# Attention slots in half slots: values of two key tiles per burst, paired products in pieces, gathers one by one, and the second SwiGLU product moved to GpSimd

## What is computed

```python
xn = _layernorm(x, axis=-1)
x = x + attn(xn) + ffn(xn)
# attn: holo_linear(x, basis, phase, amp): (x @ basis.T) @ (amp * cos(phase)).T, rank 32
#   q, k, v = holo_linear(xn), 16 heads of 16 columns; softmax(q k / 4) v; holo_linear again
# ffn: 8 experts with 352 hidden columns, the two best per token (softmax, renormalised, times 2.5)
#   silu(x @ wg) * (x @ wu) @ wd
#   plus a shared expert with 704 hidden columns on every token
```

## Time and profile before

| | |
|---|---|
| three timed runs | 1054.34, 1055.94, 1062.08 us; median 1055.94 |
| profiled execution | 1056.45 us, span 1054.6 us |
| mean granted clock of TensorE | 0.926 |
| busy over the span | TensorE 931.8 us (88%), VectorE 646.0 (61%), ScalarE 568.1 (54%), GpSimd 327.9 (31%) |

### The profile page before, as it was taken

One profiled execution on the slowest core, in us unless ns is written; L12 is line 12 of the kernel. 1 busy time (PEld: TensorE's weight loads), 2 busy tenths in 40 slices (PEclk: granted clock), 3 DMA queues, 4 the chain that ended last, 5 costly groups with the idle time before them and its releaser, 6 DMA issues.

```text
span 1054.6 us, 19404 instructions
## 1 busy us (share of the span) xinstructions
PE 931.8 (88%) x6519; PEld 624.2 (59%) x6520; DVE 646.0 (61%) x978; ACT 568.1 (54%) x892; POOL 327.9 (31%) x305
## 2 busy tenths in 40 slices
PE   5756999999999779898998998998997998998898
PEld 3446999999999624455454455444544544544546
DVE  7778644444434555765774874874875775785653
ACT  5756544444444335554663663663664664665563
POOL 2006422222222060351343253244235235135043
PEclk9856999999999856898998998998998999999899
DMA  9976454222222354445446545545465365453220
GB/s 317 377 253 191 137 164 115 73 71 70 70 70 66 94 146 127 124 119 147 126 117 174 151 111 166 147 129 142 133 154 154 108 169 134 138 122 77 48 63 21
DMA packets 94086, 140.02 MB, mean 133 GB/s; under 512 B 18200, under 2 KB 51488, under 8 KB 92992
## 3 DMA queue, kind: packets, MB, share of 16 engines
q1 hardware_dynamic: 87328, 121.25, 40.5%
q0 software_dynamic: 6480, 17.70, 5.7%
q10 hardware_dynamic: 208, 0.14, 0.0%
HBM read 79.24 MB, written 54.71 MB: 127 GB/s over the span
## 4 chain that ended last, share of the span: by engine, by line
PE 48%; issue 24%; POOL 11%; DVE 9%; ACT 3%; another core or an unknown queue 2%; DMA 2%; SPq 0%; POOLq 0%; ACTq 0%; DVEq 0%
PE bank L1253 7%; PE s_pair L1235 6%; PE st_pair L1235 6%; PE bank L1382 5%; PE bank L1444 4%; PE st_pair L1370 4%; POOL y_b L784 3%; PE bank L1348 3%; POOL h_T L767 3%; PE s_pair L1309 3%; DVE top L1773 2%; PE bank L1243 2%; PE bank L1218 2%; ACT prob L1031 1%
## 5 line engine op out<-in xcount | busy, mean ns | idle before, releaser
L1773 DVE TENSOR_REDUCE top<-s_pair 128x2 f32<-128x1024 f32 x252 | 308.5, 1224 | 144.0 <-PE s_pair L1309 122.7
L1031 ACT ACTIVATE prob<-st_pair 128x1024 f32<-128x1024 f32 x256 | 261.6, 1022 | 217.1 <-PE st_pair L1370 152.5
L767 POOL TENSOR_TENSOR h_T<-h_f,h_T 128x512 fp32r<-128x512 f32 x40 | 51.3, 1283 | 410.7 <-ACT h_T L1013 410.7
L1382 PE MATMUL bank<-prob,v_ones 128*32 128x512 f32 x1024 | 156.4, 637 | 4.6 <-issue 4.3
L745 POOL DMA_INDIRECT xg<-xn_rows,token_of x71 | 82.9, 1168 | 216.6 <-PE bank L1218 164.6
L1348 PE MATMUL bank<-xT_b,w_sh 64*128 64x512 f32 x960 | 129.5, 402 | 15.7 <-DVE h_f L1794 13.4
L1370 PE MATMUL st_pair<-q_rows,k_rows 50*128 50x512 f32 x512 | 126.3, 480 | 14.7 <-ACT prob L1031 7.5
L1309 PE MATMUL s_pair<-k_rows,q_rows 48*128 48x512 f32 x504 | 117.0, 450 | 14.4 <-DVE top L1773 7.4
L1370 PEld LDWEIGHTS st_pair<-q_rows,k_rows 50*128 50x128 f32 x512 | 51.0, 191 | 122.8 <-ACT prob L1031 78.0
L1348 PEld LDWEIGHTS bank<-xT_b,w_sh 64*128 64x128 f32 x960 | 91.1, 188 | 43.4 <-DVE h_f L1794 22.3
L1253 PE MATMUL bank<-w_exp,c_hT 128*128 (+1 forms) x639 | 94.2, 292 | 1.0 <-ACT c_y L957 1.0
(11 more groups left out here) (233 smaller groups left out, 1163.7 us busy)
## 6 DMA issues: line engine op xcount, KB each, us to landing
qk_rows<-qk_hi SPq DMA_DIRECT2D x56, 256.0 KB
q_rows<-qk_rows SPq DMA_DIRECT2D x64, 192.0 KB
k_rows<-qk_rows SPq DMA_DIRECT2D x56, 192.0 KB
expert_rows<-c_y SPq DMA_DIRECT2D x71, 128.0 KB, 1.7
xn_T_split<-x_T SPq DMA_DIRECT2D x8, 1024.0 KB, 6.5
xT_b<-xn_T_split SPq DMA_DIRECT2D x32, 256.0 KB
qk_rows<-qk_lo SPq DMA_DIRECT2D x28, 256.0 KB
x_all<-in_L_attn_x_dram SPq DMA_DIRECT2D x8, 512.0 KB, 8.1
```

The lines of the kernel that those rows point to most:

```text
L767: pool.tensor_tensor(h_T[0:m, LO, f, :], h_f[q % 2][0:m, :], h_T[0:m, HI, f, :].bitcast(F32), ALU.subtract).then_inc(p_h, 1)
L1031: act.activation(prob[kt % 2][:, 2 * jp:2 * jp + 2, :].rearrange("p j l -> p (j l)"), st_pair[:, :], ACT.Exp, scale=HD ** -0.5).then_inc(a ...
L1382: ins = pe.matmul(ot_bank[32 * j:32 * j + 32, :], v_ones[:, kt, 4 * g + j, :], prob[kt % 2][:, j, :], start=(kt == 0), stop=(kt == TPB - 1))
L1773: dve.tensor_reduce(top[g % 2][:, :, jp, qt], score_pair(b, g, v)[:, :].rearrange("p (i k) -> p i k", i=2), AX_X, ALU.max).then_inc(d_max, 1)
```

## The change

The steps are regrouped into half slots of four. `unit` now deals one whole unit to each half slot (16 to 8 per batch, FIRST = 2), and `piece` cuts it over the steps 1, 2 and 3: a pair unit into 12, 4 and 8 matmuls, a down pair (68 matmuls) into 28, 16, 18 and, in step 0 of the next half slot, 6. In steps 0 and 4 two `values` stand one behind the other; `prob` has three buffers for it, and `score` now goes ahead of `score_T` in the other steps. The projections go to steps 2 and 6.

`hidden_shared` is gone: ScalarE's `up_half` copies half of `u_bank` to `u_half`, and GpSimd's `hidden` multiplies it into `h_f`. The next unit waits for `d_ga` and `a_uh`. `hidden_high` of a unit stands behind `exponent` of step 1 of the next half slot and waits for GpSimd. The gathers have places of their own: each waits for one `score_T`. The third buffer of the transposed rows is gone; they are loaded twice instead (`load_xT` for `low_rank`, `load_xF` for the shared expert). SyncE's slot has a new order; `load_x_b` is near its end. The semaphores that guard `m_bank` follow the new order (left out below, as are the bodies of the moved functions that only change their waits).

```diff
-        xT_2 = sb("xT_b2", [P, 2, KT, L], F32R, late)
-        prob = [sb(f"prob{i}", [P, 4, L], F32, late) for i in range(2)]
+        prob = [sb(f"prob{i}", [P, 4, L], F32, late) for i in range(3)]
...
-        FIRST = 4
+        FIRST = 2
...
-        PROJECTED = [(0, 0), (0, 2), (1, 0), (1, 2)]
-        def unit(b, g, t):
-            if t % 2 == 0:
...
+        PROJECTED = [(0, 2), (0, 6), (1, 2), (1, 6)]
+        def unit(b, g, half):
+            u = g * 2 + half
+            c, j = b if u >= FIRST else b - 1, (u - FIRST) % 8
+            if j == BOTH:
+                return "odd", c, j
             if not there(c):
                 return None, None, None
-            if i < 3:
-                return (("first", c, 0), ("second", c, 0), ("both", c, BOTH))[i]
-            return (("first", "second")[i % 2], c, i // 2) if i < 12 else ("down", c, i - 12)
+            return ("pair", c, j) if j < SFT else ("down", c, j - SFT)
...
+        def for_rows(b):
+            return xT_bs[(b + 1) % 2 if b > 1 else 1]
+        def for_shared(b):
+            return xT_bs[b % 2]
...
+            def load_xF(b):
+                wait(sp, b_r, min(b + 2, NB))
+                wait(sp, b_gu, (b - 1) * SFT)
+                for a in (HI, LO):
+                    for k in range(KT):
+                        o = (a * KT + k) * L
+                        sp.dma_start(for_shared(b)[:, a, k, :].bitcast(F32), xT_dram[of(b)][:, o:o + L]).then_inc(xF_in, 16)
...
             def slot(b, g):
                 (pb, pg), (ppb, ppg), (nb, ng), (qb, qg) = after(b, g, -1), after(b, g, -2), after(b, g, 1), after(b, g, 2)
+                if there(qb) and (qb, qg) != (0, 0):
+                    load_rows(qb, qg)
                 if ppg % 2 and moved(ppb, ppg // 2):
                     load_inverse(ppb, ppg // 2)
-                if there(qb) and (qb, qg) != (0, 0):
-                    load_rows(qb, qg)
-                if g == 1 and there(b + 1):
-                    store_qk(b + 1, 2)
-                if there(b + 1) and g < 2:
-                    store_qk(b + 1, (0, 3)[g])
-                if g == 2 and there(b + 2):
-                    if b < 0:
-                        load_xT(b + 2, HI)
-                    load_xT(b + 2, LO)
-                if g == 3 and there(b):
-                    load_x_b(b)
                 if pg % 2 and moved(pb, pg // 2):
                     move_sums(pb, pg)
                     move_values(pb, pg)
+                if g == 2 and there(b + 2):
+                    load_xT(b + 2)
                 if g == 0 and there(b + 1):
-                    store_qk(b + 1, 1)
+                    store_qk(b + 1, 0)
+                if g == 1 and there(b + 1):
+                    store_qk(b + 1, 2)
+                if g == 2 and there(b - 1):
+                    store_out(b - 1, 0)
                 if g == 3 and there(b + 2):
                     store_low_rank(b + 2)
-                    load_low_rank(b + 2)
-                if g == 2 and there(b - 1) and b < NB:
-                    store_out(b - 1, 0)
                 if there(nb):
                     load_max(nb, ng)
                 if pg % 2 == 0 and moved(pb, pg // 2):
...
                     move_values(pb, pg)
                 if pg % 2 and moved(pb, pg // 2):
                     store_inverse(pb, pg // 2)
-                if g == 1 and there(b) and there(b + 2):
-                    load_xT(b + 2, HI)
-                if g == 2 and there(b - 1) and b < NB:
+                if g == 0 and there(b + 1):
+                    store_qk(b + 1, 1)
+                if g == 1 and there(b + 1):
+                    store_qk(b + 1, 3)
+                if g == 2 and there(b - 1):
                     store_out(b - 1, 1)
+                if g == 3 and there(b + 2):
+                    load_low_rank(b + 2)
+                if g == 3 and there(b):
+                    load_x_b(b)
+                    if there(b + 1):
+                        load_xF(b + 1)
...
+            def hidden(b, q):
+                wait(pool, d_ga, b * SFT + q + 1)
+                wait(pool, a_uh, lows(b, q))
+                h = h_f[q % 2][:, :]
+                pool.tensor_tensor(h, h, u_half[:, :], ALU.mult).then_inc(p_hf, 1)
...
-            def gather_batch(b):
-                if there(b):
-                    for n in range(4):
-                        gather_y(b, n)
...
+            def gather_at(b, n, g, t):
+                wait(pool, b_st, b * 32 + g * 8 + t + 1)
+                gather_y(b, n)
             for b in range(NB):
-                hidden_low(b, 0)
+                gather_at(b, 0, 0, 4)
+                gather_at(b, 1, 0, 6)
+                gather_at(b, 2, 1, 0)
+                gather_at(b, 3, 1, 2)
                 if there(b - 1):
                     ao_low(b - 1, 1)
+                hidden(b, 0)
+                hidden_low(b, 0)
+                gather_at(b, 4, 1, 7)
+                gather_at(b, 5, 2, 1)
+                gather_at(b, 6, 2, 3)
+                hidden(b, 2)
+                hidden_low(b, 2)
+                gather_at(b, 7, 2, 6)
                 for n in range(4):
                     scale_y(b, n)
-                hidden_low(b, 2)
+                hidden(b, 3)
+                hidden_low(b, 3)
                 for n in range(4, 8):
                     scale_y(b, n)
-                hidden_low(b, 3)
+                ao_low(b, 0)
                 add_pair(b)
+                hidden(b, 4)
                 hidden_low(b, 4)
                 add_y(b)
-                ao_low(b, 0)
+                hidden(b, 5)
                 hidden_low(b, 5)
-                gather_batch(b + 1)
...
+            def up_half(b, q):
+                wait(act, b_gu, b * SFT + q + 1)
+                wait(act, p_hf, lows(b, q) - 1)
+                act.activation(u_half[:, :], u_bank[:, :], ACT.Copy, scale=0.5).then_inc(a_uh, 1)
...
-                wait(act, d_hf, b * SFT + q + 1)
+                wait(act, d_hb, b + 1) if q == BOTH else wait(act, p_hf, lows(b, q))
...
+                n = b * 16 + g * 4 + kt
+                if jp == 0 and n >= 3:
+                    wait(act, b_pv, (n - 3) // 2 + 1)
...
+                    what, c, q = unit_before(b, g, t // 4)
+                    if t % 4 == 0 and what == "pair":
+                        tanh(c, q)
+                        up_half(c, q)
+                    if t == 5 and there(nb):
+                        max_rows(nb, ng)
                     if now:
                         exponent(b, g, t)
-                    if t == 1 and there(pb):
+                    if t % 4 == 0 and what == "odd":
+                        if there(c):
+                            hidden_high(c, BOTH)
+                        if there(c - 1):
+                            low_rank_o_high(c - 1)
+                    if t == 0 and there(pb):
                         o_out(pb, pg)
+                    if t == 4 and g % 2 and moved(ppb, ppg // 2):
+                        ao_high(ppb, ppg // 2)
+                    if t % 4 == 1 and what == "pair":
+                        hidden_high(c, q)
...
+            PIECES = ((0, 6), (6, 8), (8, 12))
+            DOWN_PIECES = ((0, 14), (14, 22), (22, 31), (31, 34))
...
+            DOWN_ORDER = [(0, i) for i in range(FROM_LAST)] + [(1, i) for i in range(len(DOWNS))] + [(0, i) for i in range(FROM_LAST, len(DOWNS))]
...
+            def next_score(b, g, t):
+                (nb, ng), (qb, qg) = after(b, g, 1), after(b, g, 2)
+                if t < STEPS - AHEAD:
+                    if there(nb):
+                        score(nb, ng, t + AHEAD)
+                elif there(qb):
+                    score(qb, qg, t - STEPS + AHEAD)
+            def piece(b, g, t):
+                what, c, j = unit(b, g, t // 4)
+                n = t % 4 - 1
+                if n < 0:
+                    what, c, j = unit_before(b, g, t // 4)
+                    if what == "down":
+                        down_pair(c, j, 3)
+                elif what == "pair":
+                    gate_up_shared(c, j, n)
+                elif what == "down":
+                    down_pair(c, j, n)
+                elif what == "odd":
+                    if n == 0 and there(c):
+                        gate_up_both(c)
+                    if n == 2 and there(c - 1):
+                        low_rank_o(c - 1)
             def slot(b, g):
-                now, (pb, pg), (nb, ng), (qb, qg) = there(b), after(b, g, -1), after(b, g, 1), after(b, g, 2)
+                now, (pb, pg), (nb, ng) = there(b), after(b, g, -1), after(b, g, 1)
                 for t in range(STEPS):
+                    if t % 4:
+                        next_score(b, g, t)
                     if now:
                         score_T(b, g, t)
-                    if t < STEPS - AHEAD:
-                        if there(nb):
-                            score(nb, ng, t + AHEAD)
-                    elif there(qb):
...
+                    if t % 4 == 0:
```

(48 more changed lines are left out.)

219 lines of the change are left out of this document (107 added, 112 removed).

## The result

The changed kernel took 1087.57 us (median of four runs, 1082.82 to 1093.66), the kernel before 1055.14 beside it: ratio 1.031 (95% interval 1.022 to 1.039). Predicted were 1030: the forecast was 26 us faster, the change is 32 us slower. The profiled execution has a span of 1084.0 against 1054.6, and a mean granted clock of 0.917 against 0.926.

A forecast was written before the change was run, and what follows sets the result against it. TensorE's issue order was taken to bound the steady part, with a hole in slot 0. Per batch 70.2 + 8.4 = 78.6 against 82.8; seven periods -29.8, last slots -0.7, tail +4: -26.5, so 1030 us, range 990 to 1064.

The forecast's parts named there:

- The pace of the steps: All four slots of a batch, by TensorE's issue order and engine loops: 70.2 us against 75.6 without the hole.
- The hole: Slot 0: TensorE issues slowly during eight gathers, ScalarE idles; gathers one by one were to win back 7.2 us per batch.
- the hole stays: Rival: stores, moves and down matmuls slow slot 0, not gathers; 1080, or 1055 if half hides; chance 0.13, half 0.08.
- The late load of x: Slot 3 into next slot 0: late load_x_b delays add_y, hidden and ScalarE's exponentials, costing 8.4 us per batch.
- 0 to 2 us, taken as 0: Slot 0, step 4: rows for S, issued some 4 us late behind load_xF, were to arrive about when needed.
- 78.6: Forecast batch period in us: 70.2 for the slots plus 8.4 for the late x, against 82.8 before.
- The third rival: GpSimd or the q and k rows late elsewhere too: 2 to 3 us more per batch, 1045 to 1052; chance 0.15.
- The second product: SwiGLU product moved from VectorE to GpSimd: removes TensorE's waits on h_f, 0.8 each, five per batch, within the 70.2.
- The end: Last batch's tail: add_y and hidden stand ahead of the last hidden column, about 4 us more.
- Seven times 4.2: Saving of 4.2 us per batch over seven periods, entered in the forecast as -29.8.
- The terms given for slot 0 of the kernel before: Down halves, even steps, projections and waits, summed there to 21.1 us, with the hole 28.3.

The follow-up runs named there:

- spread: The kernel before with only its eight gathers issued one by one, GpSimd's order fitted to it: 1004.3 us beside 1054.0, ratio 0.956.
- vec_rows: The changed kernel with three loads issued earlier (two of q and k rows, one of x) and the second SwiGLU product back on VectorE: 986.9 us beside 1015.4.
- rows_early: The changed kernel with the q and k rows for the second half of slots 1 and 2 loaded ahead of the projection stores: 1036.2 us beside 1054.0.
- after_third: The changed kernel as it is, run and traced a third time: 1086.8 us beside 1053.9, ratio 1.031.
- burst_again: The changed kernel with its eight gathers back in one burst, second run of that program: 1080.6 us beside 1053.9, ratio 1.026.

## Why the prediction was wrong

**The pace of the steps** ("70.2 us"). Right in kind: a clean changed kernel has a period of 73.4, spread 75.4. The burst was 1.92 where 1.89 was said. Slot by slot 17.95, 18.2, 16.5, 17.55 were said; vec_rows (with the product on VectorE) shows 18.9, 18.0, 17.3, 19.1, 3.2 us more per batch, half of it in slot 3. There the low rank product was taken as partly hidden; no run takes it apart.

**The hole** ("7.2 per batch"). Price right, by spread, and the cause as far as that the hole needs the burst. What could not be known from one trace is that the same kernel before has it in some groups and not in others. The rival "the hole stays" is out wherever gathers go one by one. By the Trainium skill, "SBUF — State Buffer", Who interferes with whom, a DMA never contends with a compute engine. The conclusion drawn from it, that spreading the gathers gives nothing, was wrong by 50 us in both groups in which it was tried. The section speaks of SBUF's ports, and what is slowed here is TensorE's issue; whether the rule fails or doesn't reach so far, no run here shows.

**The late load of x** ("8.4 us per batch"). The queue walk was right to about a microsecond, and slots 3 and 0 came out at 21.0 + 23.0 = 44.0, where 17.55 + 17.95 + 8.4 = 43.9 were said. That they agree is luck, and the term is mis-sized. ScalarE waits 4.1 us per batch behind this load, not 8.4. Taking the late x away gave 1.7 us per batch, and 1.0 on top of rows_early, because S of slot 0 then waited for its rows ("0 to 2 us, taken as 0"): moving those too gave 2.5 to 3.1. The product on GpSimd cost 1.4, and the rest was the pace of slots 3 and 0. The first rival is half right: x does land late and does block, but little is won where it doesn't.

**The step that failed: SyncE's queue in slots 1 and 2.** The prediction walked SyncE through slot 3 only. It moved the projections to steps 2 and 6 for TensorE and did not ask what `store_qk` at the end of a slot does to the `load_rows` behind it. The sum has nothing for it; by rows_early it is 8.0 us per batch in slots 1 and 2. Of the 57.6 us between 1030 and 1087.6 this one edit takes 51.4 back (1036.2). With the 8.0 the sum is 78.6 + 8.0 = 86.6, and 87.4 was measured. The third rival named the mechanism ("the rows of q and k come late elsewhere too") at 2 to 3 us; it left out that the wait also lowers the clock for the V behind it.

**The gathers beside the rows.** Priced only as a gain. By after_third and burst_again they cost 5.3 us per batch in slots 1 and 2, a part of the 8.0, and 6.8 in the last slot.

**The second product.** It was to save TensorE 0.6 to 0.8 per column. Slots 1 and 2 show nothing of it. Moved back to VectorE, it gives gate and up 5.1 us of waits between 500 and 950 us that lengthen neither slot, and saves 1.4 per batch and 9.6 at the end.

**The end** ("+4"). The last slot is 10.2 longer, and not by the `add_y` that was named: the gathers one by one are a part of it (25.9 against 19.1 with the burst), and the scalings that stand between them and the product. With the product on VectorE 0.8 to 0.9 are left.

**The arithmetic.** Seven times 4.2 is 29.4, not 29.8. The terms given for slot 0 of the kernel before make 20.6 rather than 21.1, so with the hole they come to 27.8, not 28.3, against the measured 28.4. Neither changes the forecast.

The books, by the copies of the output: ahead of the first copy -4.6 us, slots 1 to 3 of batch 0 +4.3, six periods +27.7, last batch +1.9 (its slots 0 to 2 are 8.3 shorter, its last slot 10.2 longer), 0.1 behind: +29.4, the difference of the spans.

## What to carry to other kernels

When work is moved by a few steps, walk the queue of the transfers through every slot, and ask of each store that is now later which load stands behind it. A load that is 3 us late costs the wait and, mostly, the clock of the work behind it. A gain on the engine that is the bound shows only when all loads are early: here the same regrouping was +3.1% as it stood and -2.3% with the rows of slots 1 and 2 and x moved (beside 1054), and with the third load moved too and the product back on VectorE -2.8% beside 1015.

And try the parts alone before the whole. The gathers one by one, put alone into the kernel before, gave -4.4 and -4.8% beside 1054, more than the mended whole gave there (-2.3%).

## What the runs showed of the hardware

- The same kernel took 1014 and 1054 us in two groups of runs on one chip, each group within 1.4%. By the traces the difference is in slot 0, where a burst of eight gathers runs (28.5 and 23.2 us); with the gathers one by one, 1004.3 and 1001.8 where the kernel before took 1054.
- After a wait of 2.8 to 3.9 us of TensorE the next V burst took 2.56 to 3.64 us instead of 1.92 in sixteen of eighteen cases, after 5.5 to 6.8 us 3.40 to 3.64 in all six, and after 0.6 to 1.4 us 3.03 to 3.62 in four of eighteen.
- Behind 768 KB of stores SyncE's issues of four loads took 3.0 to 4.3 us with gathers beside them and 2.0 to 2.4 without; with gathers and no such stores just ahead 1.8 to 1.9. In one pair of slots the loads took 6.8 us to land with the gathers and 5.2 without.
